# Attention in a two-layer kernel: when weighted values run on TensorE, and in which units VectorE copies and divides

## The reference

```python
# L0_attn_ref, with x of (2, 512, 512), 32 heads of width 16, 8 groups of keys and values
q = (x @ wq).reshape(b, s, NH, HD)
k = jnp.repeat((x @ wk).reshape(b, s, NKV, HD), NREP, axis=2)
v = jnp.repeat((x @ wv).reshape(b, s, NKV, HD), NREP, axis=2)
scores = jnp.einsum('bihd,bjhd->bhij', q, k) * SCALE
scores = jnp.where(causal, scores, jnp.finfo(scores.dtype).min)
attn = jax.nn.softmax(scores, axis=-1)
out = jnp.einsum('bhij,bjhd->bihd', attn, v).reshape(b, s, NH * HD)
return out @ wo
```

## Time and profile before

| | us |
|---|---|
| median of 3 runs | 963.52 |
| lowest and highest | 958.69, 964.26 |
| the profiled execution | 962.55 |
| its span, first to last instruction | 960.8 |
| TensorE busy over the span | 887.9 (92%) |
| VectorE busy | 701.5 (73%) |
| ScalarE busy | 531.8 (55%) |
| GpSimd busy | 190.8 (20%) |

### The profile page before, as it was taken

How to read it: one execution, slowest core, us unless ns; L and a number is a source line. 1 busy time by engine, 2 the same in 40 slices (tenths; PEclk the granted TensorE clock), 3 DMA queues, 4 the chain that set the end, 5 groups by cost and what they waited for, 6 DMA issues and landing times.

```text
span 960.8 us, 13838 instructions
## 1 busy us (share of the span) xinstructions
PE 887.9 (92%) x5240; PEld 680.9 (71%) x5240; DVE 701.5 (73%) x900; ACT 531.8 (55%) x704; POOL 190.8 (20%) x197
## 2 busy tenths in 40 slices
PE   3798999989889799998999999999989999999996
PEld 1565565556557577786888888688867888888885
DVE  3835788889979677788777788467887766767842
ACT  3303656666762615476666666367727766666830
POOL 3002556467647113300000000000040000000004
PEclk9798999999999989999999999889999999999999
DMA  9587466566433012115333333023312333332202
GB/s 304 173 243 149 60 108 107 67 108 109 60 93 139 12 45 72 28 37 154 99 99 99 99 94 112 23 85 107 108 27 66 107 91 92 106 109 67 66 0 88
DMA packets 40162, 91.61 MB, mean 95 GB/s; under 512 B 6944, under 2 KB 10144, under 8 KB 40096
## 3 DMA queue, kind: packets, MB, share of 16 engines
q1 hardware_dynamic: 35824, 85.23, 35.2%
q10 hardware_dynamic: 4272, 5.49, 1.7%
HBM read 76.02 MB, written 2.10 MB: 81 GB/s over the span
## 4 chain that ended last, share of the span: by engine, by line
PE 78%; DVE 9%; ACT 6%; issue 4%; DMA 1%; POOL 1%; POOLq 0%; DVEq 0%; SPq 0%; ACTq 0%
PE PS L1495 15%; PE PS L1496 14%; PE PS L1497 14%; PE PS L1811 5%; PE PS L1812 5%; PE PS L1813 5%; PE PS L1600 4%; PE PS L1632 3%; PE PS L1615 3%; DVE MX L1276 2%; ACT PT L856 2%; DMA WM<-in_WM 1%; POOL X L695 1%; ACT PL L816 1%; PE PS L1517 1%
## 5 line engine op out<-in xcount | busy, mean ns | idle before, releaser
L816 ACT ACTIVATE PL<-CODE 128x1024 f32<-128x1024 int32 x200 | 201.8, 1057 | 58.6 <-DVE ACC L1138 55.8
L1495 PE MATMUL PS<-HH,WRH 128*128 128x512 f32 x448 | 176.8, 395 | 9.7 <-DVE WRL L1150 4.3
L1496 PE MATMUL PS<-HH,WRL 128*128 128x512 f32 x448 | 176.4, 394 | 0.0
L1497 PE MATMUL PS<-HL,WRH 128*128 128x512 f32 x448 | 176.1, 393 | 0.0
L695 POOL TENSOR_TENSOR X<-X,SCR 128x512 f32<-128x512 f32 x32 | 42.5, 1342 | 570.5 <-DVE SCR L1123 570.5
L1138 DVE SCALAR_TENSOR_TENSOR ACC<-PL,ACC 128x1024 f32<-128x1024 f32 x100 | 124.4, 1244 | 8.4
L856 ACT ACTIVATE PT<-PS 128x512 f32<-128x512 f32 x160 | 85.2, 604 | 66.5 <-PE PS L1615 47.6
L1276 DVE TENSOR_REDUCE MX<-PS 128x2 f32<-128x256 f32 (+3 forms) x128 | 99.5, 817 | 18.3 <-PE PS L1602 11.3
L711 POOL TENSOR_TENSOR QS<-ident,MX 64x256 fp32r<-64x256 f32 x128 | 97.0, 758 | 65.9 <-DVE MX L1276 58.8
L1495 PEld LDWEIGHTS PS<-HH,WRH 128*128 128x128 f32 x448 | 85.3, 190 | 29.0 <-issue 5.9
L1600 PE MATMUL PS<-KS,QS 128*128 128x128 f32 (+3 forms) x256 | 83.9, 409 | 15.7 <-DVE MX L1276 14.2
(11 more groups left out here) (227 smaller groups left out, 1527.9 us busy)
## 6 DMA issues: line engine op xcount, KB each, us to landing
CODE<-in_CODES SPq DMA_DIRECT2D x50, 512.0 KB, 3.5
SCALE<-in_SCALES SPq DMA_DIRECT2D x100, 256.0 KB, 4.0
WM<-in_WM SPq DMA_DIRECT2D x12, 1024.0 KB, 5.3
QS<-FH SPq DMA_DIRECT2D x32, 128.0 KB, 4.1
QS<-FL SPq DMA_DIRECT2D x32, 128.0 KB, 5.2
X<-in_X ACTq DMA_DIRECT2D x2, 1024.0 KB, 12.4
out_x<-X ACTq DMA_DIRECT2D x8, 256.0 KB, 2.0
WF<-in_LBGU SPq DMA_DIRECT2D x14, 128.0 KB, 4.0
```

What stands on the lines that cost most here:

```text
L816: nc.scalar.activation(PL[:, n % 3], CODE[:, p % 2], ACT.Prelu, scale=scale, bias=bias, alpha=alpha).then_inc(s_plane, 1)
L1495: nc.tensor.matmul(dst, lh, rh, start=start and k == 0, stop=False)
L1496: nc.tensor.matmul(dst, ll, rh, start=False, stop=False)
L1497: ins = nc.tensor.matmul(dst, lh, rl, start=False, stop=stop and k == KC - 1)
```

## The change

TensorE issues weighted values one unit later: in odd iterations, weighted(n - 5) and weighted(n - 4). In every fourth iteration (n % 4 == 1), which has four transposed blocks, it issues three of these, then the block of weighted(n - 5) and the first of weighted(n - 4), then the fourth transposed block, then the rest of weighted(n - 4). The semaphore s_pv is raised with a unit's last block.

ScalarE's copies of even groups go from n % 8 == 4 to 5. On VectorE the copies of odd groups go from unit 2 to 4 of eight, the shuffle from 3 to 5, the two inversions from 4 and 5 to 7 and 8, the division from 6 to 9 (for the last pair in the loop, from n = 60 on, to 5, 6 and 7). The steps of the pieces go from units 0, 1, 7 to 2, 4, 6 of eight; three pieces are issued behind later stacks; one rounding moves from unit 62 to 63.

```diff
-PIECES_AT = {0: (0, 1), 5: (2,), 7: (3,), 10: (4,), 12: (5,)}
+PIECES_AT = {0: (0, 1), 5: (2,), 8: (3,), 11: (4,), 14: (5,)}
-ROUND_AT = {41: 0, 46: 1, 49: 2, 54: 3, 58: 4, 60: 5, 62: 6}
+ROUND_AT = {41: 0, 46: 1, 49: 2, 54: 3, 58: 4, 60: 5, 63: 6}
@@ step_at
-    slots = (0, 1, 7)
+    slots = (2, 4, 6)
@@ pair_at
-    return n // 8 - 1 if n >= 8 and n % 8 == unit else None
+    return (n - unit) // 8 - 1 if n - unit >= 8 and (n - unit) % 8 == 0 else None
@@ ScalarE
-                if n % 8 == 4:
+                if n % 8 == 5:
                     copy_even(act, n // TB - 1)
@@ VectorE
-                if pair_at(n, 2) is not None:
-                    copy_odd(pair_at(n, 2))
-                if pair_at(n, 3) is not None:
-                    swap_sums(pair_at(n, 3))
-                for half in range(2):
-                    if pair_at(n, 4 + half) is not None:
+                if pair_at(n, 4) is not None:
+                    copy_odd(pair_at(n, 4))
+                if pair_at(n, 5) is not None:
+                    swap_sums(pair_at(n, 5))
+                for half, unit in enumerate((5, 6) if n >= 60 else (7, 8)):
+                    if pair_at(n, unit) is not None:
                         invert(half)
-                if pair_at(n, 6) is not None:
-                    divide(pair_at(n, 6))
+                if pair_at(n, 7 if n >= 60 else 9) is not None:
+                    divide(pair_at(n, 7 if n >= 60 else 9))
@@ TensorE
-            def transposed(n):
+            def transposed(n, first=0, last=TB):
-                for jc in range(ic + 1):
+                for jc in range(first, min(last, ic + 1)):
-            def weighted(n):
+            def weighted(n, first=0, last=TB):
-                for jc in range(ic + 1):
+                for jc in range(first, min(last, ic + 1)):
-                ins.then_inc(s_pv, 1)
+                if last > ic:
+                    ins.then_inc(s_pv, 1)
-            for n in range(units + 3):
+            for n in range(units + 4):
                 if n < units:
                     scores(n)
+                if n >= 5 and n % 4 == 1 and n < units + 2:
+                    transposed(n - 2, last=TB - 1)
+                    weighted(n - 5)
+                    weighted(n - 4, last=1)
+                    transposed(n - 2, first=TB - 1)
+                    weighted(n - 4, first=1)
+                    continue
                 if 2 <= n < units + 2:
                     transposed(n - 2)
-                if n >= 3 and n % 2 == 0:
-                    for unit in (n - 4, n - 3):
+                if n >= 5 and n % 2 == 1:
+                    for unit in (n - 5, n - 4):
                         weighted(unit)
```

## The result

| | before | after |
|---|---|---|
| median, us | 963.2 (20 runs) | 965.84 (20 runs) |
| lowest and highest | 958.39, 964.5 | 964.17, 970.81 |
| the profiled execution, its span | 962.55, 960.8 | 970.81, 969.0 |

After over before is 1.0039, 95% interval 1.0027 to 1.0051. The forecast was 958.0; by the medians the change costs 2.6 us instead of gaining 4.6. The profiled execution of after is itself 5 us above its median, which has to be kept apart from what the change does.

The account below looks back on a forecast made before the run. Neither TensorE nor VectorE alone, but their hand-over order, bounds the attention loop. Start -2.1, periods -6.5, missed waits +1.0, codes +1.4, end +1.9, GpSimd -0.3: -4.6, from 962.55 to 958.0 us; range 950.5 to 965.5, forecast's own 954 to 962.

Parts of the forecast that it names:

- Start, -2.1: First scores to unit 7: the first two curve sums leave units 0 and 1, one returns in unit 2; 2.1 us saved.
- The walk, -6.5: Seven periods of eight units, 7 to 63: walked engine by engine at 23.84 us each against 24.77, 6.5 us gained.
- missed waits: Seven periods of the loop: 1.0 us taken off the gain for waits that the walk misses.
- changes of kind: Unit 1 of four on TensorE: cutting the weighted batch around the last transposed block costs 0.4 us a group.
- Rival D: Unit 1 of four: both added changes cost a full record, 0.6 us more a group, 967 us; chance 0.07.
- rival B: TensorE's batches in the steady part: the changes of kind cost nothing, 951.4 us; chance 0.22.
- 0.3 gained by GpSimd: End of the loop: the fold a unit earlier frees GpSimd earlier, 0.3 us gained (0 to 1.3).
- Queue, +1.4: SP's queue near unit 54: piece 5's codes, behind stack 14, land late for VectorE's curve sum; 1.4 us lost.
- End, +1.9: Unit 63: fold and rounding ahead of the last exponentials; 11.7 us to the last weighted value, not 9.8; 1.9 lost.
- Rival C: VectorE's copies in unit 12 and codes landing at 7.9 become new waits; 962.6 us, no change; chance 0.11.

Follow-up runs that it names:

- Run 8: Run 5 with GpSimd's two scalings of a piece two units apart and its additions two units later: 958.11 us, 0.9955 of before.
- run 11: The changed kernel with the codes of piece 5 behind stack 13, not 14, measured once more: 955.78 us, 0.9915 of before.
- run 4: The changed kernel without the cut, four transposed blocks and then three weighted ones in one batch: 960.13 us, 0.9986 of before.
- run 3: The changed kernel with GpSimd's two additions of pieces 2 and 3 two units later: 965.42 us, 1.0031 of before.
- run 2: The changed kernel with the output weights rounded on ScalarE behind unit 60, not 62: 968.06 us, 1.0063 of before.
- Run 5: Changed kernel, codes behind stack 13, output weights loaded and rounded earlier, subtraction after the last diagonal, last inversions behind unit 63's maxima: 958.68 us, 0.9934 of before.
- run 1: The changed kernel with the codes of piece 5 one stack earlier, behind stack 13, not 14: 955.47 us, 0.9927 of before.
- run 9: The changed kernel with the codes of piece 5 one stack later, behind stack 15, not 14: 976.98 us, 1.0142 of before.
- run 6: The kernel before, with output weights loaded after the last curve, rounded behind unit 60 and subtracted after the last diagonal: 959.74 us, 0.9973 of before.
- run 10: The changed kernel with TensorE's order as before, ScalarE's and VectorE's steps and codes as changed: 984.47 us, 1.0214 of before.

## Why the prediction was wrong

The sign was wrong, and the size by 7.8 us. In the two profiled executions the start gave -2.0 (forecast -2.1), the six periods to unit 55 -4.3 (-4.7), the last period +3.2 (+0.6, the codes in it), and the way from unit 63 to the landmark +7.3 (+1.9): the steps that failed are the last two. By the steps of the sum:

- *Start, -2.1.* Right: 20.42 became 18.45, at nearly the same clock.
- *The walk, -6.5 with 1.0 off for missed waits.* Right in five periods of seven, 23.1 to 24.0 against 23.84 on average. Up to unit 55 the six periods took 143.59 against 147.88, -4.3, where six sevenths of 5.5 are 4.7. The changes of kind at the cut cost 0.07 to 0.33 for both, less than the 0.4 that I took. Rival D (a whole record each, 1.0) is out; rival B (nothing) is not excluded as to this price, but its 951.4 is the farthest from what was measured. The Trainium skill's rule that a change of tiling mode drains TensorE (TensorEngine Tiling (Array Packing), Key Properties) can cost no more than that in this trace.
- *GpSimd, missing in the sum.* The period from unit 31 to 39 lost 2 to its neighbours. I walked TensorE, VectorE and ScalarE and left GpSimd out, as it is busy 20% of the span. But its diagonal stands between maxima and transposed blocks, and the moved folds bring two scalings in neighbouring units. Run 8 gives back 1.0; the wait of the first scaling for the fold, which it leaves, may be the rest, but no run tests it. The 0.3 gained by GpSimd, which the sum had, no run shows.
- *Queue, +1.4.* Right as a mechanism, and mis-sized. The codes were issued at 244.82, 13.7 after T of unit 49 (12.9 forecast), and came 3.9 later; the sum waited 2.3, 0.9 more than forecast, and 0.8 of that is the later issue. The loop lost 3.1 by it (after against run 11) and the median ten. The step that failed is that it was priced as a wait and nothing more: products at the lower clock come behind it. How much that adds varies. The last period has the late codes in runs 4, 3 and 2 too, where the sum waits 1.7, 2.6 and 2.5 us; it takes 27.54, 30.07 and 30.23 there, at mean clocks of 1.00, 0.89 and 0.89, against 25.54 at 1.00 in run 11. (Runs 2 and 3 have other waits in it as well.)
- *End, +1.9.* The chain was right up to the fourth block (10.29 for 10.3). The step that failed is what follows it. I put the last weighted value 1.4 behind that block, where before itself has 2.3 (286.02 to 288.35), and at half the clock it was 4.8. I had also not seen the 1.43 us for the diagonal of unit 63: an inversion of 1.74 us now stands between the maxima of units 62 and 63. Run 5 shows both together, by taking them away in one edit. From unit 63 to the landmark the loss is 7.3 in after's profiled execution, and 3.8 to 4.7 in runs 1, 3, 9 and 11, which have the same end and the same two stalls, but a mean clock of 0.91 there, not 0.84.
- *The sum against the profiled execution.* It took the stages behind the attention as fixed. Their rest is 640.9 to 650.4 us over kernels in which it has the same instructions, as much as all that I summed. The range had no term for that.
- *Rival C's price.* It named late copies and codes at 7.9, and priced the copies alone (7 x 0.65). With the 5.2 of the late codes for the forecast's 1.4 it would have been 966.4.

Rival C was half right: the codes were later than forecast, though not by a landing of 7.9 (it took 3.9); the copies were not late (1.6 us in the loop). No rival ended on the slower side through the codes and the end together, which is what happened.

**What the change is worth.** The two moves shorten the steady loop by 0.7 us a period and the start by 2. The codes' stack and the end of the loop give back more. With the codes one stack earlier the kernel is faster than before by 0.7 to 0.9% in two sessions, the best median measured (955.5). Runs 5 and 8 are shorter up to the landmark by another 2.6 to 5.5 us, and run 5 has the fastest single execution (949.66), but not in the median.

**What stays open** is why the clock falls where it does in the rest. That it makes the differences can be read: 610 to 635 us, after and then run 11, the last but two of the columns:

```profile
610.00:635.00 25.00, 25.00 (x141) 0.77 0.09 26
```

```profile
610.00:635.00 25.00, 25.00 (x145) 1.00 0.23 64
```

TensorE is busy all of the time in both, so no stall in that stretch lowers it. Before and run 5 have 0.73 there. The mean granted clock of two stretches, 320 to 400 and 600 to 640 us, sorts the rests:

| | rest, us | clock 320 to 400 | clock 600 to 640 |
|---|---|---|---|
| run 4 | 640.9 | 0.96 | 1.00 |
| runs 1 and 11 | 642.0 | 0.94 | 1.00 |
| run 6 | 642.9 | 0.94 | 1.00 |
| before, runs 3 and 8 | 646.9 to 647.0 | 0.96 | 0.83 |
| after and run 2 | 650.0 | 0.91 | 0.83 |
| run 5 | 650.4 | 0.91 | 0.83 |

Runs 9 (646.8) and 10 (646.2) lie between, with 0.96 and 0.87, 0.89 and 1.00. The fall at 600 us comes with late codes (after) and without them (before, runs 5 and 8), so it can't be put down to the codes alone.

The same shows over the executions of one kernel: after's three at a mean clock of 0.961 took 970.2 to 970.8 us, its six at 0.972 took 964.2 to 965.3; run 5's four at 0.984 took 949.7 to 951.5, its eight at 0.968 to 0.970 took 957.9 to 960.3. At 0.975 before took 959.5 to 961.5 (four executions) and runs 1 and 11 955.8 to 956.7 (six), so the kernel with the codes one stack earlier is faster than before at an equal mean clock too, by some 4 us. What decides between the groups the profiles do not tell. So that moving the codes one stack earlier gains ten microseconds over after is measured; 4.3 to 6.5 of them have their place up to the landmark (run 11 against run 3 and against after), and for the remainder the runs show the clock, but not what links it to the codes.

## What to carry to other kernels

Where a change moves work between engines, walk every engine that stands in a hand-over, the one that is busy 20% too, and walk the first and the last units apart from the steady part: here the steady part did what the walk said, and the edges lost more than it gained. Price a stall of TensorE above its length, since what follows it may run at the lower clock (here 3.1 us for a wait of 2.3, 15.7 for 14.0). And read each run at a landmark right behind the edited stage besides its total, because later stages can move by more than the change is worth; the mean granted clock of each execution says which ones may be set side by side.

## What the hardware showed that was not expected

- After TensorE had stood 2.03 us the granted clock was 0.75 over 252 to 258 us. After 1.43 and 2.02 us within six microseconds it was 0.50 for twelve (286 to 298), and a weighted record took 57 ns instead of 31. With waits of 0.75 and 0.36 us at the same place (run 5) it stayed at 31 ns.
- The same stalls are not always followed by as long a time at the lower clock: over the 24 us from 6 us behind T of unit 63 on, with stalls of 1.40 to 1.43 and 2.02 to 2.03 us in each, the mean clock was 0.72 in after and 0.86 in runs 1, 3, 9 and 11. The 0.14 between them are 3.4 us of full speed over 24, and after is 3.4 us longer than run 11 from unit 63 to the landmark.
- A longer stall did not cost more beyond its length in proportion: in run 9 TensorE stood 13.7 us, and units 0 to 63 took 15.7 us more than in run 11, 1.7 beyond the sum's wait of 14.0; in after it was 3.1 for 2.3, 0.8 beyond.
- The two halves of GpSimd's diagonal took 3.54 us beside VectorE's subtraction of 128 x 2048 and 1.62 us in the same place without it.
- Stages without an edit, in which TensorE is busy nearly all the time, moved by up to 9.5 us from kernel to kernel, with the clock.
